# Attention kernel: numerator and denominator in one accumulator bank, a ring of 16 probability tiles, and a strided four-tile sum on VectorE

## The reference

```
q, k, v = proj(Wq, bq) / sqrt(32), proj(Wk, bk), proj(Wv, bv)
m       = resize(mask 32x32 -> 64x64, bilinear)
attn    = softmax(q @ k^T)                # 16 (image, head) pairs, 4096 x 4096 each
fuse    = attn @ v
x1      = (Wf @ [x, fuse] + bf) * m + x * (1 - m)
edge    = relu(bn(depthwise3x3(x1)));  gate = sigmoid(fc2(relu(fc1(mean(x1)))))
o       = bn(fusion @ [x1 * gate, edge] + b)
out     = bn(balance @ depthwise3x3(o) + b) * x1
```

## Time and profile before

| | us |
|---|---|
| median of 3 runs | 4203.85 (4203.06 to 4205.12) |
| the profiled execution: its own time | 4203.13 |
| the profiled execution: its span | 4201.3 |
| TensorE busy with matmuls | 4044.0 (96%) |
| VectorE busy | 3550.1 (84%) |
| GpSimd busy | 3222.2 (77%) |
| ScalarE busy | 2339.9 (56%) |

### The profile page before, as it was taken

How to read it: one execution, slowest core, us unless ns; L and a number is a source line. 1 busy time by engine, 2 the same in 40 slices (tenths; PEclk the granted TensorE clock), 3 DMA queues, 4 the chain that set the end, 5 groups by cost and what they waited for, 6 DMA issues and landing times. The chain is left out here.

```text
span 4201.3 us, 81722 instructions
## 1 busy us (share of the span) xinstructions
PE 4044.0 (96%) x20341; PEld 1975.3 (47%) x20341; DVE 3550.1 (84%) x5350; ACT 2339.9 (56%) x4424; POOL 3222.2 (77%) x1360
## 2 busy tenths in 40 slices
PE   7979999999999999999999999999999999969797
PEld 4534444444444444444444444444444444424343
DVE  3279999999989999999899999999999999917989
ACT  1216666666656666666566666666666666641213
POOL 2429999999989999999899999999999999960000
PEclk9959999999999999999999999999999999989998
DMA  6931100110001101110111011100110000013021
GB/s 190 285 100 39 41 21 22 42 39 22 21 23 41 31 21 32 41 31 21 31 41 31 21 31 38 35 20 18 40 38 21 21 21 21 17 27 85 20 80 40
DMA packets 213798, 184.92 MB, mean 44 GB/s; under 512 B 115986, under 2 KB 140740, under 8 KB 213316
## 3 DMA queue, kind: packets, MB, share of 16 engines
q1 hardware_dynamic: 213508, 181.74, 16.2%
HBM read 122.10 MB, written 59.24 MB: 43 GB/s over the span
## 5 line engine op out<-in xcount | busy, mean ns | idle before, releaser
L761 ACT ACTIVATE prob<-st 128x512 f32<-128x512 f32 x4096 | 2154.3, 601 | 1309.3 <-PE st L626 1048.6
L819 DVE TENSOR_REDUCE block_max<-mx 128x1 f32<-128x512 f32 x4096 | 2562.0, 683 | 343.4 <-PE mx L633 330.0
L490 POOL TENSOR_TENSOR prob_sum<-prob_sum,prob 128x1024 f32<-128x1024 f32 x768 | 1929.3, 2512 | 127.5 <-POOL prob_sum L490 100.4
L633 PE MATMUL mx<-keys,max_queries 96*128 96x512 f32 x4096 | 1648.0, 426 | 38.2 <-DMA keys<-k_scratch 27.8
L626 PE MATMUL st<-queries,keys 97*128 97x512 f32 x4096 | 1574.5, 411 | 1.6 <-ACT prob L761 1.5
L490 POOL TENSOR_TENSOR prob_sum<-prob 128x1024 f32<-128x1024 f32 x448 | 1067.8, 2383 | 253.1 <-ACT prob L761 253.1
L633 PEld LDWEIGHTS mx<-keys,max_queries 96*128 96x128 f32 x4096 | 777.8, 191 | 737.3 <-DVE block_max L819 564.8
L645 PE MATMUL acc<-prob,values 128*32 128x512 f32 x8192 | 1039.7, 602 | 0.0
L626 PEld LDWEIGHTS st<-queries,keys 97*128 97x128 f32 x4096 | 776.7, 190 | 520.6 <-ACT prob L761 282.2
L645 PEld LDWEIGHTS acc<-prob,values 128*32 128x32 f32 x8192 | 194.4, 108 | 427.1 <-issue 226.1
L665 PE MATMUL dacc<-prob_sum,ones 128*32 128x512 f32 x2048 | 273.0, 605 | 9.2 <-POOL prob_sum L490 9.2
(11 more groups left out here) (119 smaller groups left out, 1213.8 us busy)
## 6 DMA issues: line engine op xcount, KB each, us to landing
max_queries<-q_scratch SPq DMA_DIRECT2D x384, 64.0 KB, 1.9
queries<-q_scratch SPq DMA_DIRECT2D x384, 64.0 KB, 2.0
keys<-k_scratch SPq DMA_DIRECT2D x168, 128.0 KB, 2.5
x<-in_x SPq DMA_DIRECT2D x18, 512.0 KB, 4.1
q_scratch<-high SPq DMA_DIRECT2D x32, 256.0 KB, 4.4
k_scratch<-high SPq DMA_DIRECT2D x16, 512.0 KB, 4.9
q_scratch<-low SPq DMA_DIRECT2D x32, 256.0 KB, 5.0
k_scratch<-low SPq DMA_DIRECT2D x16, 512.0 KB, 4.9
```

The lines of the kernel that those rows point to most:

```text
L490: ops.tensor_tensor(psum[k][:, :, :], a[:, :, :], prob[(first + i) % RING][:, :, :], ALU.add).then_inc(added[own], 1)
L633: nc.tensor.matmul(mx[bank(j, p)][:, :], qm[p][:, h, ns * P:(ns + 1) * P], kk[gp][0:SPLIT, h, blk * CH:(blk + 1) * CH], start=True, stop=T ...
L761: nc.scalar.activation(prob[s % RING][:, h, :], st[bank(i, p)][:, :], ACT.Exp).then_inc(exp_done, 1)
L819: nc.vector.tensor_reduce(bmax[p][:, j // MB, j % MB:j % MB + 1], mx[bank(j, p)][:, :], AX.X, ALU.max).then_inc(mx_taken, 1)
```

## The change

In attention:

- The bank `dacc` is gone. `sums` writes into `acc`, after the unit's last `V` and after ScalarE has copied it out (`copy_num`, both halves, two copies of 64x512). The first `V` of the next unit waits for `copy_den` (one copy of 128x512).
- The freed bank is a fourth one for the max blocks (MAX_BANKS).
- `prob` is one tensor with RING = 16 tiles. VectorE sums group 3 by four `tensor_reduce` of four tiles each, over a strided axis (`add_up`; each gives 128x256 outputs from 1024 inputs, neighbouring inputs of one sum 4096 bytes apart). Its three additions, `take_num` and `take_den` are gone; `invert` has a small reduce ahead of the reciprocal.
- GpSimd does its 19 additions in an order in which two chains are interleaved (`chain_order`), and adds the two halves of the numerator ahead of the multiplication.
- ORDER is another string: 149 letters again, with 64 `m`, 64 `s`, 16 `V` and 5 `S` in both. Maximal runs of `V` and `S` without another letter between: 15 before, 11 now. BLOCKS_AHEAD is 32 for 29, SCORES_AHEAD 14 for 13.

Outside it: the first upsampling of the mask moves from the end of `project_phase` to the start of `image_phase`, and four weight tensors of the image phase (1.66 MB) are stored to HBM in `project_phase` and loaded again at the start of `image_phase`, where TensorE waits for all of them.

```diff
-RING = 8
-ORDER = ("msmsmsVmsmsmsmsVsmsmsmsmsmVmsmsmsmsmsVVVsmsmsmssmsmsmsVVsmmsmssSVsmssmmsVV"
-         "mssmsmmssmsmSmssmsmmVmssmsmmVmsmssmmVmmsmssmSmsmsmsmVmssmsmmVSsmsmsmsSsmsms")
-SCORES_AHEAD = 13
-BLOCKS_AHEAD = 29
-TAKE_NUM, TAKE_DEN, INVERT = 24, 32, 40
-ADD_AFTER = [43, 51, 54]
-NUM_AFTER, DEN_AFTER = 6, 13
-SCALE_AFTER = 4
+MAX_BANKS = 4
+RING = 16
+ORDER = ("smsmsmsmsmsmsmsmsmVsmsmsmsmsmsmsmsmVsmsmsmsmsmsmsVssmsmsVVVsmssmmsmsmsmsms"
+         "VVVsmmssVVVsmsmsmsmsmmssmsmVsmsmsmmVmmsmmssmVmmsmsmsmVmsmssmmmsmsmssmsSSSSS")
+SCORES_AHEAD = 14
+BLOCKS_AHEAD = 32
+INVERT = 59
+ADD_AFTER = [52, 55, 61, 62]
+NUM_AFTER, DEN_AFTER = 5, 19
+SCALE_AFTER = 17
+def chain_order():
+    chains = [k for k, size in enumerate(GROUPS) if k not in BY_VECTOR and size > 1]
+    order = [(k, i) for k in chains for i in range(1, GROUPS[k])]
+    for k, after in zip(chains, chains[1:]):
+        if GROUPS[k] > 2:
+            order.remove((after, 1))
+            order.insert(order.index((k, GROUPS[k] - 1)), (after, 1))
+    return order
+PIECES = [(k, h, half) for k in BY_VECTOR for h in range(2) for half in range(2)]
...
+        def add_up(dve, u, k, h, half):
+            first, last = GROUP_END[k] - GROUPS[k], GROUP_END[k] - 1
+            dve.wait_ge(sums_done, SUMS * u + k // 2 + 1)
+            dve.wait_ge(exp_done, TILES * (u + 1) + 2 * last + h + 1)
+            cols = slice(half * CH // 2, (half + 1) * CH // 2)
+            tiles = prob[:, first % RING:last % RING + 1, h, cols].rearrange("p t n -> p n t")
+            nc.vector.tensor_reduce(psum[k][:, h, cols], tiles, AX.X, ALU.add).then_inc(added[True], 1)
...
             def values(u, gp, q):
                 if q == 0:
-                    pe.wait_ge(num_ready, u + 1)
+                    pe.wait_ge(den_ready, u + 1)
...
             def sums(u, i):
                 if i == 0:
-                    pe.wait_ge(den_ready, u + 1)
+                    pe.wait_ge(num_out, 2 * (u + 1))
...
+            def copy_num(v):
                 act.wait_ge(num_ready, v + 1)
                 act.wait_ge(v_done, QUADS * (v + 2))
-                nc.scalar.copy(num_even[:, :], acc[0:2 * HD, :]).then_inc(num_half, 1)
+                for a in range(2):
+                    nc.scalar.copy(num_part[a][:, :], acc[2 * HD * a:2 * HD * (a + 1), :]).then_inc(num_out, 1)
+            def copy_den(v):
+                act.wait_ge(den_stored, 16 * (v + 1))
                 act.wait_ge(sums_done, SUMS * (v + 2))
-                nc.scalar.copy(den_even[:, :], dacc[0:2 * HD, :]).then_inc(den_half, 1)
+                nc.scalar.copy(den[:, :], acc[:, :]).then_inc(den_ready, 1)
...
             def scale(v):
+                pool.wait_ge(num_out, 2 * (v + 1))
+                pool.wait_ge(fuse_ready, v + 1)
+                nc.gpsimd.tensor_tensor(num[:, :], num_part[0][:, :], num_part[1][:, :], ALU.add).then_inc(num_ready, 1)
...
+            sp.dma_start(flat(late["wf"]), scratch["wf"][:, :]).then_inc(weights_back, 16)
+            load(0, 0, 0)
+            load_mask(0)
+            load(0, 1, 1)
+            for w in IMAGE_WEIGHTS[1:]:
+                sp.dma_start(flat(late[w]), scratch[w][:, :]).then_inc(weights_back, 16)
```

More of the change, by code:

```diff
@@ L176, in _, with flat @@
                 take(i)
+def flat(t):
+    if len(t.shape) == 3:
+        return t[:, :, :].rearrange("p a b -> p (a b)")
+    return t[:, :, :, :].rearrange("p a b c -> p (a b c)")
 def upsample(nc, dve, small, mask, step, before):
@@ L272, in _ @@
             load(0, 1, 1)
-            sp.dma_start(small[0][:, :, :].rearrange("p h w -> p (h w)"),
-                         dram["mask"].rearrange("b a h w -> (b a) (h w)")[0:1, :].broadcast_to((P, 1024))
-                         ).then_inc(mask_loaded, 16)
+            for w in IMAGE_WEIGHTS:
+                sp.dma_start(scratch[w][:, :], flat(keep[w])).then_inc(put_away, 16)
             with sp.Fori(0, B) as b:
@@ L421, in attention_phase @@
         qm = [sb(f"max_queries{p}", [SPLIT, 2, CH], F32R) for p in range(2)]
-        prob = [sb(f"prob{r}", [P, 2, CH]) for r in range(RING)]
+        prob = sb("prob", [P, RING, 2, CH])
         psum = [sb(f"prob_sum{r}", [P, 2, CH]) for r in range(len(GROUPS))]
@@ L656, in sums @@
                         pe.wait_ge(added[j in BY_VECTOR], ADDS[j in BY_VECTOR] * (u + 1) + adds_until(j, GROUPS[j] - 1))
-                    src = [psum[k + a] for a in range(2)]
+                    src = [psum[k + a][:, :, :] for a in range(2)]
                 else:
@@ L660, in sums @@
                     pe.wait_ge(exp_done, TILES * (u + 1) + 2 * t + 4)
-                    src = [prob[(t + a) % RING] for a in range(2)]
+                    src = [prob[:, (t + a) % RING, :, :] for a in range(2)]
                 for a in range(2):
@@ L880, in image_phase @@
         xf = [sb(f"xf{p}", [P, 2 * CT, CH]) for p in range(2)]
-        mask = keep["mask"]
+        mask = sb("mask", [P, HH, WW])
+        late = image_weights(sb)
+        keep = {**keep, **late}
         small = [sb("m32", [P, 32, 32]), sb("q32", [P, 32, 32]), sb("m64", [P, 32, WW])]
@@ L1273, in image @@
                     dve.wait_ge(mask_loaded, 16 * (b + 1) + 16)
-                    upsample(nc, dve, small, keep["mask"], mstep, NM * (b + 1))
+                    upsample(nc, dve, small, mask, mstep, NM * (b + 1))
                 deform(b, NCH - 1, 1, nxt=0)
@@ L1284, in _ @@
             dve.sem_inc(edge_step, EARLIER * EDGE_DVE)
-            dve.sem_inc(mstep, NM)
+            dve.wait_ge(mask_loaded, 16)
+            upsample(nc, dve, small, mask, mstep, 0)
             for t in range(CT):
@@ L1294, in _, with image_weights @@
             image(B - 1, False)
+def image_weights(sb):
+    late = {w: sb(f"{w}T", [P, kts, ots * P]) for w, ots, kts in WEIGHTS if w in IMAGE_WEIGHTS}
+    late["diag"] = sb("diag", [P, CT, EDGE_PE, P])
+    return late
 def build(nc, dram, out):
@@ L1313, in build @@
         }
-        for w, ots, kts in WEIGHTS:
-            if w not in PROJECTIONS:
-                keep[w] = sb(f"{w}T", [P, kts, ots * P])
         scratch = {
@@ L1329, in build @@
         with ExitStack() as first:
-            weights = {w: first.enter_context(nc.sbuf_tensor(f"{w}T", [P, kts, ots * P], F32))
-                       for w, ots, kts in WEIGHTS if w in PROJECTIONS}
+            early = lambda name, shape: first.enter_context(nc.sbuf_tensor(f"first_{name}", shape, F32))
+            weights = {w: early(f"{w}T", [P, kts, ots * P]) for w, ots, kts in WEIGHTS if w not in IMAGE_WEIGHTS}
+            weights.update(image_weights(early))
             setup_phase(nc, dram, {**keep, **weights})
```

141 lines of the change are left out of this document (61 added, 80 removed).

## The result

| | before | after |
|---|---|---|
| median of 4 runs, us | 4203.45 (4202.53 to 4205.12) | 4127.73 (4126.87 to 4128.21) |
| span of the profiled execution | 4201.3 | 4125.6 |
| a unit in the middle | 53.64 | 52.22 |
| TensorE, VectorE, GpSimd, ScalarE busy in it | 53.64, 48.44, 48.85, 34.38 | 52.22, 47.28, 47.14, 34.89 |

The ratio of the times is 0.9819, 95% interval 0.9802 to 0.9836: 76 us faster. The prediction said 4122 us, 4085 to 4175, and 0.88 for faster; the time is 5.7 us above the number.

The account below looks back on a forecast made before the run. The prediction took TensorE's own order of letters as the bound. Its terms, -92 - 2 + 1.5 - 4 + 15.5 = -81 us, took the profiled 4203.13 to 4122 us, range 4085 to 4175.

Parts of the forecast that it names:

- What bounds the kernel: Attention's middle units: TensorE's own order of letters is the bound; only 0.6 us of a 53.64 us unit is waiting.
- The string's price: TensorE's letters in attention: fewer clusters save 1.3 us a unit, with waits 1.49; over 62 units -92 us.
- The shared bank: Sums and numerator sharing acc in attention: 0.05 us of waits a unit, at the V that needs copy_den.
- The max banks: Max blocks in attention: nine run two blocks ahead of VectorE, four banks hold that, no wait found.
- The strided sum: VectorE's four reductions a unit in attention: 1.13 us each, all hidden at that price.
- the fourth rival: VectorE's strided reductions: the stride doubles an input's time, 2.2 us a sum, 12 us more, 4134; chance 0.12.
- The third rival's threshold: Attention's row of maxima comes late when strided sums are dear; slower from about 2.6 us each, 4276 at 2.93; chance 0.09.
- Taking the two-operand steps from VectorE: GpSimd additions in attention: each beside a two-operand VectorE step takes 3.16 us, otherwise 2.36 to 2.38; GpSimd's work is hidden.
- GpSimd: Its work in an attention unit: 48 us, new addition 1.28, hidden with 4 us of cover.
- Start of attention: Upsampling leaves VectorE there: -2 us, limited by the last store; more max blocks and a score ahead: +1.5.
- Last two units: End of attention, GpSimd the bound: fewer slowed additions and waits, less the new addition; -4 us.
- Image phase: Its start: mask load, upsampling of 13.1 us and wf's subtraction precede the first product, uncovered; +15.5 us.

Follow-up runs that it names:

- the run over neighbours: The changed kernel with all four strided reductions taken over four neighbouring elements of one tile instead: 4126.8 us, ratio 0.9820.
- The reordered run: The changed kernel with its image phase loading the mask first, subtracting wf's identity before upsampling, and first products waiting for wf alone: 4114.2 us, ratio 0.9795.
- the first string of 8 clusters: The changed kernel with another ORDER of 8 clusters and 13 further letters, and sums and inversion behind other max blocks: 4208.6 us, ratio 1.0012.

## Why the prediction was right

- **What bounds the kernel.** Right, and shown from both sides: 4 clusters more cost 1.33 us a unit, and 3.3 us less on VectorE give nothing. VectorE's room is small, though: 2.0 us more on it cost 2.4 a unit.
- **The string's price.** Right: 1.42 us a unit instead of 1.49. The letters' prices hold to 0.01, and waits came to 0.52 in place of 0.45. The 62 units gave 88, not 92. Not foreseen: the two units at the loop's ends are 3.2 us shorter beyond that. The shorter stops are 1.8 of it; why they shrank was not tried.
- **The shared bank.** Right, 0.05 a unit forecast and 0.9 us of the whole measured, about nothing.
- **The max banks.** The walk found no wait with four, and TensorE's products show none. Its reason, that nine blocks run two ahead and four banks hold that, understated the need: three banks cost 267 us, where this reasoning allowed 20 to 75. It left out the time that a bank is away between the product and the reduction's end; that this is the whole reason is argued.
- **The ring.** No run changes the 16 tiles alone, so what they are worth is open.
- **The strided sum.** This term was mis-sized. The prediction took 1.13 "since the max block is the same instruction at one input per element"; it measured 2.03, since every input lies more than 16 bytes from the last. Even over neighbours it takes 1.21, twice a max block's 0.60, so the 0.07 that the prediction split off as overhead doesn't show. For the total the price didn't matter, less than the 12 us that the fourth rival gave it (0 to 1 by the run over neighbours). Of the prediction's own price and this rival's, the one held likelier was the wrong one.
- **The third rival's threshold.** The row of maxima is not what decides. Five sums of 2.0 us, as much as four of 2.5, already cost 2.4 us a unit, at max banks, and make the kernel 73 us slower than before; by the prediction's working the row is 0.4 us late there, and the change turns slower only at 2.6. Neither the size nor the mechanism is right, and the clock's part was not in it.
- **Taking the two-operand steps from VectorE.** The prediction counted only their 0.8 us on GpSimd, as hidden. With GpSimd's additions interleaved they would have cost 763 us, with pauses 169. The step that fell short is "a faster VectorE or GpSimd can give back 0.6 us at most": true of the old string, but it says nothing of what the new order needs.
- **GpSimd.** Right: 47.1 us of work a unit (48 forecast), all additions at 2.4, the new one 1.29 (1.28 forecast).
- **Start of attention.** -2 was forecast, -0.6 came. The last store stood in the way, issued at 220.96 (220.67 before). The 1.5 us for more max blocks ahead didn't come: the first unit is 2.3 us shorter, 0.9 more than the usual 1.42.
- **Last two units.** -4 was forecast, -0.7 came (one unit's 1.4 more in the stretch up to the last negated maximum, less 0.7 behind it). The new addition stands behind the eighteenth of GpSimd's, so that the last unit's numerator copies wait for it and TensorE for them: 3.46 us at 3650.38. The prediction had seen this wait in the middle, as hidden, and not at the end, where TensorE has no other work. That this makes up the 3.3 us is argued, not tested.
- **Image phase.** Right: 16.1 instead of 15.5, with the mechanism named. The reordered run took 13.5 of it back.

The terms together: -81 forecast, -75.7 measured. The string gave 4 less, the last units 3.3, the start and the image phase behind its first product 1.4 each, its start 0.6; the loop's ends gave 3.2 more and the first unit 2.4. So misses of 10.7 one way and 5.6 the other partly cancel, and that the total lies as near as 5.7 us is in part luck; the string's 88 of 92 is not.

## What to carry to other kernels

Price an engine's own instruction order from starts in its timeline, count the prices for the new order, and check every cover by its place; that gave a unit to 0.07 us. But ask of each part of a change not only what it gives but what the others need it for: the fourth bank and the single-operand sums, with all else but the merged clusters, gave 0.1 us a unit, and without the one the new order was 267 us slower, without the other 169 to 763. And count a buffer from the moment it is given to the moment it is back, travel included, not by the consumer's pace. And where an engine's wait is priced, look at the clock behind it: a wait of 1.4 us a unit went with units longer by 2.4 here.

## What the runs showed of the hardware

- A two-operand step on VectorE can wait through several GpSimd additions that follow each other without a pause: 12.2 us on average, against 1.6 where GpSimd pauses 0.16 us between dependent additions.
- A VectorE reduction of 1024 fp32 inputs from SBUF takes 1.2 us with neighbours and 2.0 with inputs 16 or 4096 bytes apart; 256 outputs or one make no difference.
- An engine's loop jump can cost it 2.2 us (ScalarE, two units a round, in the first string of 8 clusters). The changed kernel, where ScalarE idles there, never shows it; where it shows, units alternate.
- A reduction starts 0.43 us or more behind its product, so that a bank is away for over 1.1 us though the reductions follow every 0.60.
- Where TensorE had waited 1.4 to 1.9 us, the granted clock was 0.61 to 0.68 over a stretch of 4 us there or right behind; behind a wait of 7.3 us it was 0.50 over 4 us; it was 1.00 in the changed kernel's middle, where it never waits.
